# The gram matrices of a delta-rule chunk by one 128-row product in place of four 32-row ones

## The reference, cut to what matters

```python
H, D = 4, 32
def step(S, ch):                       # S: one 32 x 32 state per batch and head
    Q, K, V, bt = ch                   # one chunk of C tokens
    Kb, Vb = K * bt, V * bt
    A = eye(C) + tril(einsum('bhcd,bhed->bhce', Kb, K), -1)
    T = solve_triangular(A, eye(C), lower=True)
    W, U = T @ Kb, T @ Vb
    St = S.swapaxes(-1, -2)
    mid = U - W @ St
    O = Q @ St + einsum('bhcd,bhed->bhce', Q, K) * M @ mid     # M: lower triangle
    S_new = S + mid.swapaxes(-1, -2) @ K
    return S_new, O
```

## Time and profile before

| what | value |
|---|---|
| median of 3 runs | 1664.27 us (1662.66 to 1668.79) |
| the profiled execution: its own time | 1668.01 us |
| its span in the trace | 1666.2 us |
| PE busy, DVE busy, ACT busy | 82%, 73%, 48% of the span |
| mean granted TensorE clock | 0.919 |
| the delta pass in the trace | 1085 to 1409 us |

### The profile page before, as it was taken

One profiled execution on the slowest core, in us unless ns is written; L12 is line 12 of the kernel. 1 busy time (PEld: TensorE's weight loads), 2 busy tenths in 40 slices (PEclk: granted clock), 3 DMA queues, 4 the chain that ended last, 5 costly groups with the idle time before them and its releaser, 6 DMA issues. The chain is left out here.

```text
span 1666.2 us, 36566 instructions
## 1 busy us (share of the span) xinstructions
PE 1364.3 (82%) x13255; PEld 965.2 (58%) x13255; DVE 1212.4 (73%) x2728; ACT 806.8 (48%) x1447; POOL 117.0 (7%) x76
## 2 busy tenths in 40 slices
PE   0668998999999999999989888535777776677876
PEld 0556775666666666666657667433445544466665
DVE  6785126877777777777767777648877884799997
ACT  0564325666666656666646666411122211566663
POOL 2000000000000000000021222200000000122221
PEclk9778999999999999999999999877889899798897
DMA  8000003433333333333322444560322001111111
GB/s 228 1 0 0 5 5 92 117 115 112 113 112 114 112 112 110 113 113 114 114 71 71 125 120 135 147 237 3 113 105 96 29 29 40 46 57 57 51 51 31
DMA packets 122258, 142.22 MB, mean 85 GB/s; under 512 B 8768, under 2 KB 78752, under 8 KB 121120
## 3 DMA queue, kind: packets, MB, share of 16 engines
q1 hardware_dynamic: 118704, 134.81, 25.8%
q10 hardware_dynamic: 3440, 5.79, 1.0%
HBM read 106.49 MB, written 34.08 MB: 84 GB/s over the span
## 5 line engine op out<-in xcount | busy, mean ns | idle before, releaser
L969 ACT ACTIVATE glu_a<-moe_a,b1s 128x512 f32<-128x512 f32 x256 | 176.3, 689 | 226.1 <-PE moe_a L898 226.0
L915 PE MATMUL moe_y<-glu_a,w2s 128*128 128x512 f32 x512 | 261.3, 592 | 0.3 <-DVE glu_a L1019 0.2
L1002 DVE TENSOR_SCALAR b_raw<-b_raw 128x512 f32<-128x512 f32 x256 | 109.3, 427 | 143.3 <-ACT b_raw L974 143.0
L896 PE MATMUL moe_a<-x_hi,w_hi 128*128 128x512 f32 x256 | 192.5, 752 | 5.4 <-DVE w_lo L1028 5.4
L974 ACT ACTIVATE b_raw<-moe_b,b1s 128x512 f32<-128x512 f32 x256 | 176.0, 687 | 2.6 <-PE moe_b L898 1.1
L1019 DVE TENSOR_TENSOR glu_a<-glu_a,gate_row 128x512 f32<-128x512 f32 x256 | 175.7, 686 | 0.0
L1011 DVE SCALAR_TENSOR_TENSOR glu_a<-glu_a,b_raw 128x512 f32<-128x512 f32 x256 | 175.3, 685 | 0.1
L915 PEld LDWEIGHTS moe_y<-glu_a,w2s 128*128 128x128 f32 x512 | 96.2, 188 | 23.9 <-DVE glu_a L1019 2.1
L898 PE MATMUL moe_b<-x_hi,w_lo 128*128 128x512 f32 x256 | 102.1, 399 | 0.0
L898 PE MATMUL moe_a<-x_hi,w_lo 128*128 128x512 f32 x256 | 101.9, 398 | 0.0
L896 PE MATMUL moe_b<-x_hi,w_hi 128*128 128x512 f32 x256 | 101.9, 398 | 0.0
(11 more groups left out here) (256 smaller groups left out, 2749.0 us busy)
## 6 DMA issues: line engine op xcount, KB each, us to landing
gate_row<-gate_scratch SPq DMA_DIRECT2D x256, 256.0 KB, 3.1
kq_scratch<-kq_out SPq DMA_DIRECT2D x32, 256.0 KB, 3.5
kq_in<-kq_scratch SPq DMA_DIRECT2D x8, 1024.0 KB, 7.3
acc<-in_L_attn_inputs SPq DMA_DIRECT2D x8, 512.0 KB, 10.0
xq_scratch<-qT SPq DMA_DIRECT2D x16, 256.0 KB, 2.0
v_scratch<-v_out SPq DMA_DIRECT2D x16, 256.0 KB, 2.3
k_scratch<-k_out SPq DMA_DIRECT2D x16, 256.0 KB, 2.8
k_rows_scratch<-k_rows SPq DMA_DIRECT2D x16, 256.0 KB, 3.2
```

The costliest lines, as they stand in the source:

```text
L896: pe.matmul(bank[:, :], w1_hi[:, e, s, :], hi, start=True, stop=False)
L915: pe.matmul(bank, w["w2"][:, e, :], glu_a[e % 4][:, :], start=(e == 0), stop=(e == E - 1), skip_group_check=True).then_inc(down, 1)
L969: act.activation(glu_a[e % 4][:, :], ps_a[u][:, :], ACT.Gelu_apprx_sigmoid, bias=w["b1"][:, 0, e:e + 1]).then_inc(a_glu, 1)
L1002: dve.tensor_scalar(b_raw[u][:, :], b_raw[u][:, :], 1.0 + LIMIT, 1.0 - LIMIT, ALU.min, ALU.max).then_inc(b_cut, 1)
```

## The change

The keys of a group are copied into a second buffer, `blocks`, in which the 32 keys of head h of a chunk stand in the 32 columns of block h on the 32 partitions of head h, and everything else is zero. With that as 128 x 128 weights, one product with the 64 columns of `kq_in` gives the gram matrices of all four heads of a chunk, in the same place of `ps_g` as before. There are two such buffers, of 128 x 4096 elements each. POOL clears them once, one ahead of `eye` and one behind it. ACT fills the blocks by `spread_k(g, h)`, one activation for each head, of 32 partitions x 1024 elements, with new semaphores `blanked` and `k_spread`. PE waits for `k_spread` ahead of a group's first quarter. SP loads the next keys into `k_in` after the spread and no longer after the gram product. To make room, tiles of the earlier passes are given back ahead of `delta_pass`; that changes addresses and no instruction.

```diff
@@ two_blocks_kernel
-            conv=keep("convs", [P, 3, TAPS, DIM]),
...
+        middle = ctx.enter_context(ExitStack())
...
         project_pass(nc, w, kept)
+        middle.close()
         delta_pass(nc, w, kept)
@@ delta_pass
+        blocks = [sb(f"k_blocks{i}", [P, NCH, HEADS, CH]) for i in range(2)]
+        blanked, k_spread = sem("k_blanked"), sem("k_spread")
...
                 def load_k(g):
                     if g >= 2:
-                        sp.wait_ge(grammed, QUARTERS * (g - 1))
+                        sp.wait_ge(k_spread, HEADS * (g - 1))
...
                 fill = Chain(pool, eye_filled, 0)
+                pool.memset(blocks[0][:, :, :, :], 0.0).then_inc(blanked, 1)
                 fill.step(pool.memset(eye[:, :, :], 0.0))
                 fill.step(pool.affine_select(out=eye[:, :, :], in_=eye[:, :, :], compare_op=ALU.not_equal, fill=1.0,
                                              base=0, pattern=[[1, CH], [-1, CH]], channel_multiplier=0))
+                pool.memset(blocks[1][:, :, :, :], 0.0).then_inc(blanked, 1)
                 pool.memset(idle_in[:, :], 0.0).then_inc(idle_set, 1)
...
                 def gram(g, quarters):
                     if quarters[0] == 0:
                         pe.wait_ge(k_loaded[g % 2], 48 * (g // 2 + 1))
+                        pe.wait_ge(k_spread, HEADS * (g + 1))
...
                         for i in range(8):
-                            for rows in heads():
-                                mm = pe.matmul(ps_g[quarter % 2][rows, i, :, :], k_in[g % 2][rows, 8 * quarter + i, :],
-                                               kq_in[g % 4][rows, :, 8 * quarter + i, :], start=True, stop=True)
+                            n_at = 8 * quarter + i
+                            mm = pe.matmul(ps_g[quarter % 2][:, i, :, :],
+                                           blocks[g % 2][:, n_at, :, :].rearrange("p h t -> p (h t)"),
+                                           kq_in[g % 4][:, :, n_at, :], start=True, stop=True)
                         mm.then_inc(grammed, 1)
...
+                def spread_k(g, h):
+                    if h == 0:
+                        act.wait_ge(blanked, min(g + 1, 2))
+                        act.wait_ge(k_loaded[g % 2], 48 * (g // 2 + 1))
+                        if g >= 2:
+                            act.wait_ge(grammed, QUARTERS * (g - 1))
+                    rows = heads()[h]
+                    act.activation(blocks[g % 2][rows, :, h, :], k_in[g % 2][rows, :, :], ACT.Copy)\
+                       .then_inc(k_spread, 1)
...
+                        if g + 3 < GROUPS and c >= 2:
+                            for h in range(2 * c - 4, 2 * c - 2):
+                                spread_k(g + 3, h)
...
                 set_eye(1)
+                for g in range(2):
+                    for h in range(HEADS):
+                        spread_k(g, h)
                 copy_gram(0, range(QUARTERS))
+                for h in range(HEADS):
+                    spread_k(2, h)
                 copy_gram(1, range(QUARTERS))
```

More of the change, by code:

```diff
@@ L192, in two_blocks_kernel @@
             ident16=keep("ident16", [P, P], BF16),
-            conv=keep("convs", [P, 3, TAPS, DIM]),
-            wb=keep("wbs", [P, HEADS, HD]),
             wo=keep("wos", [P, DIM]),
@@ L197, in two_blocks_kernel @@
             wd=keep("wds", [P, 3, DIM]),
[L198 to L201, removed]
             upper=keep("upper", [P, 2, CH]),
[L203 to L209, removed]
             minus_half=keep("minus_half", [P, 1]),
@@ L220, in two_blocks_kernel, with until_delta @@
             gate=scratch("gate_scratch", [EXPERTS, TOKENS]),
+        )
+        middle = ctx.enter_context(ExitStack())
+        def until_delta(name, shape, dt=F32):
+            return middle.enter_context(nc.sbuf_tensor(name, shape, dt))
+        w.update(
+            conv=until_delta("convs", [P, 3, TAPS, DIM]),
+            wb=until_delta("wbs", [P, HEADS, HD]),
+            st=until_delta("st", [P, NSUB, 6]),
+            mean=until_delta("mean", [P, NSUB]),
+            rs=until_delta("rs", [P, NSUB]),
+            rr=until_delta("rr", [P, NSUB]),
+            conv_hi=until_delta("conv_hi", [P, 3, TAPS, DIM], F32R),
+            conv_lo=until_delta("conv_lo", [P, 3, TAPS, DIM], F32R),
+            wb_hi=until_delta("wb_hi", [P, HEADS, HD], F32R),
+            wb_lo=until_delta("wb_lo", [P, HEADS, HD], F32R),
+            stats=[until_delta(f"stats2_{name}", [P, NSUB]) for name in ("mean", "var", "diff", "tmp")],
+            rs2=until_delta("rs2", [P, NSUB]),
+            shift=until_delta("shift2", [P, NSUB]),
         )
```

## The result

| | before | after |
|---|---|---|
| median, runs | 1665.85 us of 9 (1662.66 to 1672.05) | 1676.72 us of 9 (1671.84 to 1679.77) |
| ratio of the runs, with its 95% interval | | 1.0056 (1.0039 to 1.0073) |
| the profiled execution: its own time, span | 1668.01, 1666.2 us | 1677.04, 1675.3 us |
| mean granted clock | 0.919 | 0.914 |
| PE, DVE, ACT busy | 82%, 73%, 48% | 83%, 72%, 50% |

The changed kernel is 0.56% slower. The range of the prediction (1643 to 1681) holds it; the forecast of 1665.7 us is 11 us too low, and the time is 2.7 us outside the forecast's own range of 1658 to 1674. The gram quarters and the supply of instructions came out near their numbers, and so did the scans by the runs of the experiments. The start of the delta pass did not.

What follows compares the result with a forecast made beforehand. DVE bounds chunks 2 and 3; in chunks 0 and 1 it waits on PE, read as short of instructions. 1668.0 - 6.6 (scans) + 8.0 (start) = 1669.4, or 1665.7 us against the median; own range 1658 to 1674, wide 1643 to 1681.

Steps and rivals of the forecast that it cites:

- The quarter: Gram quarter on PE: 16 products bound by 128-column weight loads take 1.9 us in place of 0.92, 3.4 at the lower clock.
- Supply of instructions: PE in chunks 0 and 1: breaks come from supply, 127 pairs per 3.84 us; 231 pairs a chunk need 7.0 us, ending breaks.
- Rival D: PE's breaks aren't supply and stay on top of the 18.0 us pairs: 15 us on the forecast, 1680; chance 6%.
- The sign that went with it: Scans: few "issue" breaks of PE in chunks 0 and 1, DVE's gram-copy waits near 2.5 us a group.
- A pair at the high clock: Chunks 0 and 1 of a group at full clock: 18.0 us with PE as the bound; group 0 18.7 us.
- The clock in the scans: Chunks 0 and 1: 20.3 us at the lower level cost half, 10.2 us; two thirds kept, 6.8 us.
- the sum of 115.5: Chunks 0 and 1, six groups: 18.7 + 5 x 18.0 + 6.8 us against 122.1 before, 6.6 us won.
- The spreads in the scans: ACT's spreads behind chunks 2 and 3: hidden except 0.4 us ahead of a pair; chunks 2 and 3 unchanged.
- The start: Start of the delta pass: zeros, spreads, copies and longer quarters delay group 1's transposition, 8 us lost.
- Its two bounds, 5.3 and 12.4: Start's loss in us: 5.3 with only the first two quarters at the lower clock, 12.4 with the whole start there.
- Rival B: PE's clock falls more in its own bound stretch, start wholly at the lower clock: +19 us, 1683; chance 20%.

Runs made afterwards that it cites:

- e4: Changed kernel, but groups 0 and 1 get gram matrices by the old products, no spreads ahead of them, zeros behind `eye`: 1660.84 us, ratio 0.9959 to before.
- e9: Changed kernel with its zeros and spreads in the start, but groups 0 and 1 use four 32-row products a chunk, keys read from the blocks: 1667.58 us, ratio 0.9999.
- e1: e4 with 32 moving columns in place of 64 from group 2 on (output incomplete): quarter 1.87 us, 1673.29 us in one run.
- e2: e4 with 64 columns of weights in place of 128 from group 2 on (heads 0 and 1 only, output incomplete): quarter 1.15 us, 1650.35 us in one run.
- e3: Kernel before the change, with gram products of only two of four heads from group 2 on (output incomplete): 1657.01 us in one run.
- e7: e4 without the idle products right ahead of gram quarters in the scans, 10 fewer a group: 1673.46 us, ratio 1.0050 to before.
- e5: Changed kernel plus idle products of 512 columns in the start, 24 ahead of the first quarter and three behind each quarter: 1686.59 us, ratio 1.0108 to before.
- e8: Changed kernel's order of zeros, spreads and copies, with two 64 x 64-weight products a chunk everywhere, zeros half the size: 1656.67 us, ratio 0.9939 to before.
- e6: e4 with blocks of two heads, two products of 64 rows x 64 weight columns a chunk: 1652.17 us, ratio 0.9912 to before.

## Why the prediction was right or wrong

The times of the runs make an account, each step one ratio less another, of some 1666 us (with an uncertainty of some 3 us for the first step, which has one interval, and of 4 to 5 for the others, which have two):

| step | ratios | us | in the traces |
|---|---|---|---|
| new products and spreads in the scans (before to e4) | 1 to 0.9959 | -6.8 | pairs -0.3 (e4), -3.1 (after); start 28.45 to 27.04: -1.4 |
| zeros and spreads ahead of the first quarter (e4 to e9) | 0.9959 to 0.9999 | +6.7 | start 27.04 to 32.14: +5.1 |
| 128-column products in the start (e9 to after) | 0.9999 to 1.0056 | +9.5 | start 32.14 to 40.74: +8.6 |
| all | 1.0056 | +9.3 | |

Point by point, by the prediction's own steps:

- **The quarter** at 1.9 us: right, 1.89, and for the reason given. The slope over weight columns of the earlier trace rows was the right row to choose by. e1 and e2 show that columns of weights set it and moving ones don't. At the lower clock it was forecast at 3.4 and is 3.44. The 114 ns a pair, and the same quarter with half of the moving columns in e1, also stand against the rule of the Trainium skill that the prediction weighed (TensorE: Matmul & The Clock Gate, The mechanism): loads over all rows do overlap with matmuls over all rows.
- **Supply of instructions**: right in the main. The breaks of all groups fell from 34 us to about 10 with the change and to 19 in e3. Rival D falls. The sign that went with it was missed: DVE's waits for the gram copy were to be near 2.5 us a group and are 3.9.
- **A pair at the high clock** at 18.0 us: 18.79 and 18.36 in groups 2 and 3. Group 0 was forecast at 18.7 and took 17.75. PE became the bound, as e7 shows at 0.95.
- **The clock in the scans**: the amount at the lower level was forecast too low, and its price too high. By (1 - clock) x 2 x length, groups 1 to 5 had 9.1 + 0 + 0 + 6.7 + 9.5 = 25.3 us at the lower level. The prediction took the 20.3 us of before and let a third of them go; none went. At half of each it would be 12.6 us. But the two pairs at 1.00 have a mean of 18.6 us, so that five would take 92.9, and groups 1 to 5 took 101.2: the term is 8.3 us, or 0.33 us for each at the lower level, beside a forecast of 6.8. Against the sum of 115.5, group 0 gave 0.9 back, the length of five pairs at the high clock added 2.9 and the clock 1.5: that is the 118.9 measured, a win of 3.1. These shares are of one execution. Pairs at 1.00 took 17.6 to 19.0 us in e4, e5 and e9, three kernels with the same scans as after, whose sums were 121.8, 124.2 and 114.1 us. In the runs of e4 the win is 6.8, beside a forecast of 6.6; as the interval goes from 4.0 to 9.8, that it comes so close is luck in part.
- **The spreads in the scans**: hidden, as said. Chunks 2 and 3 took 15.7 us in five of the six groups and 16.4 in one.
- **The start** is the step that failed. Its chain was right: spreads, then the copies, then quarters on two `ps_g`. Of its two bounds, 5.3 and 12.4, I took 8, because the clock had been 0.69 there before. That row was read as a property of the place. With the same place and the same spreads, the products of e8 and e9 had 0.62 and 0.57 and those of the change 0.50, so it belonged to the products too. The term came out at 12.3, the bound with every quarter at the lower clock. The transposition was forecast between 1119 and 1126 and came at 1127.68, of which 1.8 is the later start of the pass.
- **Rival B** named this case: slower by over 0.5% as soon as the scans win less than 4 us beside a start that loses 12.4. In the profiled execution they won 3.1 beside 12.3. Its place was half wrong: the loss lies in the start and not in the scans. With 12.3 in place of 8, the prediction's sum is 1670.0, +0.3%; the rest up to the measured 0.56% is about 4 us. In the runs the start costs 16.2 us (6.7 + 9.5), in the traces 13.7 from e4 to after. The 2.5 us between the two are within the uncertainty.

Open too is why the clock stays low with 128-column products. e9 and e8 show that it comes with them and not with the late start or the spreads, and e5 that three idle products behind each quarter don't help. No run lets them begin at the higher clock, as the idle products of e5 ended 5 us ahead of them. No run separates the share of time that PE loads from the share that it streams.

## What to carry to other kernels

Merging small products saves instructions only up to the point where the wider weight load is the new bound: for a product with few moving columns, price it by the columns of its weights, and try the middle size (64 here) before the full one. A stage that is started once, ahead of everything, deserves its own form: the same edit won about 0.4% in the scans and lost 1% at the start, where nothing hides it. Idle products that are to raise the clock for a stage should reach up to its first product: in e5 the clock that they had raised was gone after a gap of 5 us (no run here closes that gap, so what it would give is not shown). When a stretch's granted clock is taken over from the kernel before, ask whether the new instructions keep it up; if not known, take the bound.

## What the runs showed of the hardware that was not expected

- A TensorE that is busy in every record can stay at 1.2 GHz: 27.54 us of gram products without a gap in the records (whose ends are modelled), granted clock 0.50 throughout. The Trainium skill (TensorE: Matmul & The Clock Gate, Part 1) describes the gate as following how busy PE has been; here the busy time of the trace was no guide to it.
- Idle products of 512 columns in a row raised the clock, and the same products between load-bound quarters didn't: 23 of them from 1087.94 had it at 1.00 from 1091.0 on (e5), while three behind each quarter of the same start left it at 0.50, 3.5 us a quarter. In the scans, without those beside the quarters (e7), the mean clock fell from 0.86 to 0.79.
- Two 64 x 64 products on different rows and columns together take as long as one with 128 rows and 64 columns of weights: 1.15 us for 32 MATMULs (e6) and for 16 (e2).
- A copy on ACT of 1024 elements takes 1.05 us on 32 partitions and on 128 alike. The row of the spreads in the changed kernel (min/median/max ns), beside the earlier trace rows:

```profile
L1604 ACT ACTIVATE k_blocks<-k_in x32: 1038/1053/1057, 1094.7 to 1330.2; 32x1024 f32<-32x1024 f32 x32
```
